# Perceiver block on one core: the FFN weights' quantising moved from attention 2 to attention 1, VectorE's additions one step later

## The reference, cut to what matters

```
x = x + xattn0(layernorm(x), ctx, mask, Wq, Wk, Wv, Wo)   # attention 1: 64 rows, 16 heads, 6272 keys
x = x + attn0(layernorm(x), qkv, wo)                      # 64 x 64 with rope
x = x + moe(layernorm(x), router, gate, up, down)         # 8 experts
x = x + xattn1(layernorm(x), ctx, Wq, Wk, Wv, Wo, bo)     # attention 2 over the same 6272 keys, then a small one
x = x + delta(layernorm(x), ...)                          # convolutions, delta rule, gates
x = x + ffn(layernorm(x), W_in, b_in, W_out, b_out)
...
def quantize_w8_per(w, axis):                             # of ffn: W_in and W_out
    amax = jnp.clip(jnp.max(jnp.abs(w), axis=axis, keepdims=True), 1e-08, None)
    scale = 127.0 / amax
    w_q = jnp.clip(jnp.round(w * scale), -128.0, 127.0) / scale
```

## Time and profile before

| what | us |
|---|---|
| median of 3 runs (406.82 to 411.14) | 407.27 |
| the profiled execution | 406.98 |
| its span, first to last instruction | 405.1 |
| attention 1, first to last `score` and `pv` | 19.26 to 170.1 |
| rope attention, experts, second fold | 171 to 208 |
| attention 2, the same | 208.45 to 350.8 |
| what follows, to the end | 351 to 405.1 |

### The profile page before, as it was taken

How to read it: one execution, slowest core, us unless ns; L and a number is a source line. 1 busy time by engine, 2 the same in 40 slices (tenths; PEclk the granted TensorE clock), 3 DMA queues, 4 the chain that set the end, 5 groups by cost and what they waited for, 6 DMA issues and landing times.

```text
span 405.1 us, 11383 instructions
## 1 busy us (share of the span) xinstructions
PE 383.4 (95%) x4529; PEld 280.0 (69%) x4529; DVE 276.8 (68%) x715; ACT 287.2 (71%) x568; POOL 256.4 (63%) x207
## 2 busy tenths in 40 slices
PE   6988899999999999989999999998999999999996
PEld 3435677777777778954955767776777768867843
DVE  2796788888887776566767766676776666454544
ACT  3478768888888887646439988999888987534240
POOL 2489988999975659201007989999999879030000
PEclk9899999999999999999999999999999999999999
DMA  8899979999999999990006999999999999700000
GB/s 308 323 256 154 198 142 199 160 184 208 182 190 212 228 201 155 354 391 2 3 2 105 203 190 191 196 186 194 173 194 211 183 195 179 302 2 2 3 1 5
DMA packets 188389, 68.55 MB, mean 169 GB/s; under 512 B 183200, under 2 KB 183984, under 8 KB 187440
## 3 DMA queue, kind: packets, MB, share of 16 engines
q1 hardware_dynamic: 188048, 66.77, 82.1%
q10 hardware_dynamic: 288, 1.05, 0.7%
HBM read 21.90 MB, written 0.03 MB: 54 GB/s over the span
## 4 chain that ended last, share of the span: by engine, by line
PE 47%; POOL 19%; DMA 11%; DVE 9%; ACT 6%; issue 5%; SPq 0%; POOLq 0%; DVEq 0%; ACTq 0%
PE ps L522 16%; POOL halves L594 14%; PE ps L490 13%; DMA probsT<-halves 10%; DVE probs L641 3%; PE ps L1106 2%; PE ps L502 2%; PE ps L768 2%; ACT probs L559 2%; DMA moe<-in_ctxT 2%; ACT halves L566 2%; PE ps L1214 1%; PE ps L828 1%; PE ps L942 1%; PE ps L773 1%
## 5 line engine op out<-in xcount | busy, mean ns | idle before, releaser
L594 POOL TENSOR_TENSOR halves<-probs,halves 128x896 f16<-128x896 f32 x84 | 160.8, 1924 | 36.1 <-ACT halves L566 34.9
L522 PE MATMUL ps<-ctxN,probsT 128*128 128x128 f16 x2352 | 148.6, 219 | 5.9 <-DMA probsT<-halves 5.8
L522 PEld LDWEIGHTS ps<-ctxN,probsT 128*128 128x128 f16 x2352 | 139.0, 98 | 20.7 <-issue 10.4
L490 PE MATMUL ps<-ctxT_parts,GT_parts 128*128 128x512 f16 (+1 forms) x660 | 142.9, 353 | 3.7 <-DVE negmax L641 3.5
L559 ACT ACTIVATE probs<-probs,shifted 128x896 f32<-128x896 f32 x112 | 115.5, 1031 | 7.2 <-DVE shifted L646 7.2
L490 PEld LDWEIGHTS ps<-ctxT_parts,GT_parts 128*128 128x128 f16 x660 | 59.9, 98 | 54.4 <-DVE negmax L641 5.4
L566 ACT CAST halves<-probs 128x896 f16<-128x896 f32 x93 | 85.9, 923 | 0.1
L654 DVE SCALAR_TENSOR_TENSOR U<-U,alpha,ps 128x128 f32<-128x128 f32 x112 | 38.7, 345 | 60.4 <-PE ps L522 60.3
L641 DVE CUSTOM_DVE_ANT_0 probs<-ps,maskb,negmax 128x896 f32<-128x896 f32 x56 | 67.5, 1206 | 3.7 <-POOL halves L594 3.3
L641 DVE CUSTOM_DVE_ANT_0 probs<-ps,zero,negmax 128x896 f32<-128x896 f32 x56 | 67.5, 1206 | 2.1 <-POOL halves L594 1.6
L556 ACT ACTIVATE alpha<-negmax 128x1 f32<-128x1 f32 x96 | 28.3, 295 | 36.8 <-DVE negmax L641 36.3
(11 more groups left out here) (369 smaller groups left out, 381.2 us busy)
## 6 DMA issues: line engine op xcount, KB each, us to landing
moe<-in_ctxT SPq DMA_DIRECT2D x7, 448.0 KB, 7.5
moe<-in_mask SPq DMA_DIRECT2D x6, 448.0 KB, 9.9
moe<-in_gateT SPq DMA_DIRECT2D x2, 1024.0 KB, 9.2
moe<-in_upT SPq DMA_DIRECT2D x2, 1024.0 KB, 11.0
moe<-in_downT SPq DMA_DIRECT2D x2, 1024.0 KB, 12.6
moe<-in_fir_long SPq DMA_DIRECT2D x1, 2048.0 KB, 10.5
probsT<-halves SPq DMA_TRANSPOSE x93, 4.8
wv<-in_wv SPq DMA_DIRECT2D x2, 512.0 KB, 6.8
```

The source lines that it names most:

```text
L490: ins = pe.matmul(ps[:, 2 * b + h, 0:width], GT_parts[:, g_part, r * P:(r + 1) * P], ctxT_parts[:, keys:keys + width], start=(g_part == 0 ...
L522: ins = pe.matmul(ps[:, bank, 0:D], probsT_parts[:, b, p_part, k * P:(k + 1) * P], ctxN_parts[:, at:at + D], start=(p_part == 0 and c_part ...
L594: eng.tensor_tensor(halves_of(L, n)[:, 1, :], probs[:, n % BUFS, :], halves_of(L, n)[:, 0, :], ALU.subtract).then_inc(lower_of(L, n)[0], 1)
```

## The change

POOL's eight operations move from attention 2 (steps 12 to 40, every fourth) to attention 1 (steps 35 to 49, every second). For that the weights are loaded at steps 14 and 22 and `wqT` and `wkT` of the next fold (512 KB each) at 36 and 40, where the FFN weights (256 KB each) were; DVE takes the maxima in steps 32 and 33 and the scales in step 34 of attention 1; `wqi` and `wqo` get memory of their own, which costs one of the 7 buffers of `halves`. And `ADD_LAG` becomes 7.

```diff
-BUFS, TURNED_BUFS, HALF_BUFS = 4, 6, 7
-PV_LAG, ADD_LAG = 5, 6
+BUFS, TURNED_BUFS, HALF_BUFS = 4, 6, 6
+PV_LAG, ADD_LAG = 5, 7
...
-        wqi = late(P, FT, D)
-        wqo = late(P, FT, D)
+        wqi = sb("wqi", [P, FT, D])[:]
+        wqo = sb("wqo", [P, FT, D])[:]
...
-        WEIGHTS_AT = {14: ("in1", w_qT, "wqT1"), 22: ("in1", wkT[:], "wkT1"), 30: ("out0", wv[:], "wv0"),
-                      34: ("small_attn", a_w[:], "a_w"), 36: ("ffn", win[:], "win"), 38: ("out0", wo[:], "wo0"),
-                      40: ("ffn", wout[:], "wout"), 44: ("delta", d_w[:], "d_w"), 46: ("delta", w1s[:], "w1s")}
+        WEIGHTS_AT = {14: ("ffn", win[:], "win"), 22: ("ffn", wout[:], "wout"), 30: ("out0", wv[:], "wv0"),
+                      34: ("small_attn", a_w[:], "a_w"), 36: ("in1", w_qT, "wqT1"), 38: ("out0", wo[:], "wo0"),
+                      40: ("in1", wkT[:], "wkT1"), 44: ("delta", d_w[:], "d_w"), 46: ("delta", w1s[:], "w1s")}
...
+                if 35 <= n < 51 and n % 2 == 1:
+                    quantise_weights((n - 35) // 8, (n - 35) // 2 % 4)
...
-                        if 12 <= n < 44 and n % 4 == 0:
-                            quantise_weights((n - 12) // 16, (n - 12) // 4 % 4)
...
-            flash_dve(dve, 0, {1: partial(g_lower_dve, dve, 0, slice(4 * P, 8 * P), 5)})
+            flash_dve(dve, 0, {1: partial(g_lower_dve, dve, 0, slice(4 * P, 8 * P), 5),
+                               32: partial(weight_maxima, 0), 33: partial(weight_maxima, 1), 34: weight_scales})
```

More of the change, by code:

```diff
@@ L1409, in _ @@
             pool.wait_ge(sem("ctxT_ready"), 1)
[L1410 to L1429, removed]
             def quantise_weights(k, stage):
@@ L1443, in quantise_weights @@
                     pool.tensor_tensor(q, q, back, ALU.mult).then_inc(sem("f_wq"), 1)
+            ctxT_upper(1)
+            ctxT_lower(1)
+            for n in range(STEPS):
+                if not on_pe(0, n) and not on_vector(0, n):
+                    lower(pool, 0, n)
+                denominators(pool, 0, n)
+                if n > (CH - 1) * RT:
+                    last_denominator(pool, 0, n - 1)
+                if n == 1:
+                    mask(1)
+                if 35 <= n < 51 and n % 2 == 1:
+                    quantise_weights((n - 35) // 8, (n - 35) // 2 % 4)
+                c, part = 2 + (n - POOL_FROM) // 6, (n - POOL_FROM) % 6
+                if n >= POOL_FROM and c < CH:
+                    if part == 0:
+                        ctxT_upper(c)
+                    if part == 2:
+                        ctxT_lower(c)
+                    if part == 4:
+                        mask(c)
+            last_denominator(pool, 0, STEPS - 1)
             def keep_o1():
@@ L1615, in _, with weight_maxima, weight_scales @@
             dve.wait_ge(sem("cleared"), 3)
-            flash_dve(dve, 0, {1: partial(g_lower_dve, dve, 0, slice(4 * P, 8 * P), 5)})
+            def weight_maxima(i):
+                loaded(dve, "ffn")
+                dve.tensor_reduce(wamx[:, i * FT:(i + 1) * FT], (win, wout)[i][:], AX, ALU.max,
+                                  apply_absolute_value=True).then_inc(sem("f_maxima"), 1)
+            def weight_scales():
+                dve.wait_ge(sem("f_maxima"), 2)
+                seq(dve.tensor_scalar(wamx[:], wamx[:], 1e-8, None, ALU.max))
+                seq(dve.reciprocal(wsc[:, 0, :], wamx[:]))
+                seq(dve.tensor_scalar(wsc[:, 0, :], wsc[:, 0, :], 127.0, None, ALU.mult))
+                dve.reciprocal(wsc[:, 1, :], wsc[:, 0, :]).then_inc(sem("f_scales"), 1)
+            flash_dve(dve, 0, {1: partial(g_lower_dve, dve, 0, slice(4 * P, 8 * P), 5),
+                               32: partial(weight_maxima, 0), 33: partial(weight_maxima, 1), 34: weight_scales})
             turn_u_dve(dve, 0)
             project_dve(dve, 0)
[L1619 to L1622, removed]
             loaded(dve, "par")
@@ L1682, in _ @@
                                   ALU.mult).then_inc(sem("s_probs"), 1)
[L1683 to L1686, removed]
             dve.wait_ge(sem("a_given"), A_GIVEN["out"])
```

## The result

The changed kernel takes 411.27 us (median of 20 runs, 410.31 to 412.15), against 406.98 (20 runs). The ratio is 1.0109, with a 95% interval of 1.0096 to 1.0122: 1.1% slower, and 2.1 us above the range that was forecast. The profiled execution took 412.15, with a span of 410.4; that of before had a span of 405.1.

The account below looks back on a forecast made before the run. PE was taken to bound attention 1's second half, while attention 2 had little to spare anywhere, its queue as slow as PE or slightly slower. Terms -2.8 + 0.9 - 0.6 + 0.5 + 0.8 = -1.2 gave 406.0 us, range 402.6 to 409.2.

Parts of the forecast that it names:

- the ends: End of each attention: later additions make pv(53) and pv(52) wait for DVE; +0.45 each, +0.9 us, ends 0 and +1.6.
- the relief: Attention 2: eight quantising operations leave POOL, so PE loses less; -2.8 us, ends 0 and -4.8.
- rival 2: Attention 2: the transposition queue is and stays the bound at 2.41 us, relief worth nothing; 408.9 us, chance 0.16.
- Rival 3: Attention 1, steps 37 to 45: 512 KB loads delay the transpositions behind them, up to 4.7 us; 410.0 us, chance 0.08.
- the prediction's own sign for it: Attention 2: PE's steps staying at 2.41 us would show the forecast wrong and point to rival 2.
- The loads: Attention 1, steps 36 and 40: 512 KB loads delay queued transpositions and PE's pv; +0.8 us, ends 0 and +4.7.
- Score 17: Early in attention 1: its wait for a late DVE maximum goes with the later additions; -0.6 us, ends 0 and -0.8.
- Maxima and scales: Attention 1, steps 32 to 34: added DVE work delays PE; +0.5 us, ends 0 and +2.2.
- POOL's 12 us in attention 1: Quantising added to attention 1 fits POOL's 15.3 us of idle time; 0 us, ends -0.2 and +1.0.
- The cover that the prediction named: Attention 1: earlier maxima give back 0.7 us; without them the last quantising, before step 50's `lower`, would cost 1.05.
- One buffer less: One `halves` buffer fewer: reuse after six steps, 13.9 us, leaves enough room; costs nothing.

Follow-up runs that it names:

- experiment 2: The kernel before with ADD_LAG raised from 6 to 7 and nothing else: 409.89 us, ratio 1.0074 to the kernel before.
- 3: The changed kernel with two additions, 48 and 49, done in iteration 55, so the last additions stand as with lag 6: 407.44 us, ratio 1.0011.
- 8: The changed kernel with additions caught up in iteration 55, 512 KB loads back at 14 and 22, steps 19 and 35 of attention 2 turned on PE: 403.44 us.
- 12: As 8, with only the quantising put back into steps 12 to 40 of attention 2: 402.79 us, ratio 0.9897 to the kernel before.
- experiment 1: The changed kernel with ADD_LAG back at 6, all else as changed: 412.02 us, ratio 1.0139 to the kernel before.
- 9: The changed kernel with additions caught up in iteration 55 and, in attention 2, step 52's transposition issued only after that of 50 landed: 407.56 us, ratio 1.0007.
- experiment 4: The changed kernel with the 512 KB loads back at steps 14 and 22, the 256 KB ones at 18 and 26: 410.12 us, ratio 1.0089.
- experiment 6: The kernel before with only the upper part transposed by DMA in attention 2 and read twice by PE: 402.32 us, one run.

## Why the prediction was wrong

It said 406.0, no change; the kernel is 1.1% slower. Two terms of its sum failed, the ends by 2.7 us and the relief by 2.5, and one, pv(50), was missing; neither of the two alone would have brought the time out of its range. It gave 0.06 to a kernel slower by over 1%, and saw for that only rivals 2 and 3 together; it came by rival 2 and the ends. By its own steps:

- **The additions at the ends: +0.9, measured +3.6** (1.62 and 2.00; experiments 2 and 3). This is the step that failed in its mechanism. The prediction named pv(53) behind `turned_lower` of 55 and pv(52) behind that of 54, and worked each out from the times of before. It did not follow pv(51), whose addition 49 crosses `turned_lower` of 53, and so it missed that the wait closes a loop through PE: turn 53, ACT, `turned_lower`, addition 49, pv(51), and the same again for turn 55 and addition 51. Its upper end, 1.6 for both attentions, is what the first alone cost.
- **The relief of POOL: -2.8, measured 0** (8 against 12; within the scatter of C also experiment 1 against before), and -0.3 in the steps of attention 2 between the two profiles. This is the second step that failed. Rival 2 was right: the queue is the bound and stays it, and the prediction's own sign for it came, steps of 113.13 / 47 = 2.41. It took the 2.41 of 52 issues for 2.38 plus pauses caused by POOL. The pauses were there, and 3.2 us of them went, but the issues took as much longer, and it is still 125.22 us for 52.
- **pv(50) of attention 2: not in the sum, +1.0.** It comes with the lag (2, 3 and 9), not with the quantising (1), and only where the queue is full. Against the other runs with lag 6 (4.60 to 4.66) it is 0.6 to 0.7. Why the lag brings it is open.
- **The loads: +0.8, measured +1.1** (experiment 4), at pv(37) as named, and at no other. It came by the landing: the issue of wqT took SP 0.57, no more than a small load, where the prediction reckoned 1.10. Rival 3 at 4.7 was far too high.
- **Score 17: -0.6, measured -0.7**, by the mechanism given.
- **Maxima and scales: +0.5, measured +0.6** against the lag alone (score 36 to 37: 2.87, and 2.31 in experiment 2), and 2.2 with lag 6 (experiment 1). The two profiles show 0 by luck: the wait of pv(29) for DMA, 0.6 with its refilling, went at the same place, and no term had it. It is not in every execution: experiment 6, whose attention 1 is that of the kernel before, has 2.38 there. One size was off: VectorE's small operations, put at 0.2 each, took up to 1.87 us while GpSimd worked.
- **POOL's 12 us in attention 1: 0, measured 0** in the changed kernel, and 1.0 at pv(50) with lag 6. The cover that the prediction named was the lag.
- **One buffer less: nothing**; not tried alone, and no run shows a cost.

The forecast of 405.8 plus 2.7 for the ends, 2.5 for the relief, 1.0 for pv(50) and 0.3 for the loads, less 0.5 at score 37 (the maxima and scales 0.1 more, the wait for DMA 0.6 less) and 0.1 for score 17, is 411.7 for the profiled execution, which had 412.15 with the 0.57 at its start.

## What to carry to other kernels

Where a step is put off by one iteration, write out the last iterations for every product, and follow each wait through the other engines until it comes back to the one that waits: a loop that pipelining hides in the middle is paid in full at the end. Before an engine is relieved, ask what stands behind it: with a queue at its own rate behind it, the relief was worth nothing here, and the way to know is to unload the queue, not the engine. Parts of one change cover for each other: here the lag paid for the maxima, the quantising and, once the queue had room, 2.4 us in attention 2, so undoing it alone gave nothing back (412.02), though it mended both ends. The shortest times (402.79 and 402.92, which can't be told apart) came with the lag kept, its ends mended and the queue unloaded, once with the quantising put back and once without.

## What the runs showed of the hardware

- A `tensor_scalar` on 128x8 floats on VectorE takes 0.17 us with GpSimd idle, and took 1.5 to 1.87 where it began 0.06 to 0.45 us into a `lower` of GpSimd, ending with that `lower` each time; one that began within 0.01 us of a `lower` took 0.16 (changed kernel, 106.06). The reciprocal on a tile of that size beside it took 0.20 each time.
- On GpSimd a power with tensor exponents costs 1.68 us on 128x8 and 0.55 on 128x1.
- Transpositions of 458,752 bytes land 1.5 to 4.0 us apart in attention 2 of the changed kernel. The longest gaps, 3.7 to 4.0, came at steps 6, 20, 34 and 48, at 11, 25 and 39, and at 15, 29 and 43, each 14 steps apart; nothing tried here tells why.
